# First feed-forward layer of a two-layer network on one core: 68 dense tiles against 24 dense tiles and 39 expert slots in DRAM

## The reference, cut to what matters

```python
probs = softmax(x @ Wr)                       # 8 experts
routing_weights, selected = top_k(probs, 2)   # not renormalised
C = einsum('tk,tke->te', routing_weights, one_hot(selected, 8))
expert_out = vmap(swiglu)(x, Wg, Wu, Wd)      # swiglu: silu(x@wg) * (x@wu) @ wd, 176 hidden columns
moe_out = einsum('te,eth->th', C, expert_out)
shared = swiglu(x, Sg, Su, Sd)                # 704 hidden columns
out = moe_out + sigmoid(x @ Wsg) * shared     # then x = x + tanh(g_ffn[0]) * out
```

## Time and profile before

| | us |
|---|---|
| runs | 876.75, 870.18, 870.32; median 870.32 |
| the profiled execution, device time | 869.0 |
| its span, from first to last instruction | 867.3 |
| TensorE busy in the span | 781.8 (90%) |
| VectorE, ScalarE, GpSimd busy | 566.6, 314.5, 159.2 |

### The profile page before, as it was taken

How to read it: one execution, slowest core, us unless ns; L and a number is a source line. 1 busy time by engine, 2 the same in 40 slices (tenths; PEclk the granted TensorE clock), 3 DMA queues, 4 the chain that set the end, 5 groups by cost and what they waited for, 6 DMA issues and landing times.

```text
span 867.3 us, 13423 instructions
## 1 busy us (share of the span) xinstructions
PE 781.8 (90%) x4612; PEld 634.5 (73%) x4627; DVE 566.6 (65%) x1022; ACT 314.5 (36%) x507; POOL 159.2 (18%) x211
## 2 busy tenths in 40 slices
PE   3887888799999999999997999976699999999994
PEld 2575766688888888888884555545588888888883
DVE  4877778454654574367546898983355876868764
ACT  2220211223423343342234878756143423324221
POOL 2977877300000000021100111111010000000000
PEclk9999999999999999999998999996599999999998
DMA  7221321000000000001001122200000000000000
GB/s 279 73 91 49 104 67 30 1 1 1 1 0 0 0 0 0 0 0 33 19 1 46 54 69 75 60 31 13 1 1 1 2 24 0 0 24 0 24 1 25
DMA packets 22134, 26.09 MB, mean 30 GB/s; under 512 B 5328, under 2 KB 17744, under 8 KB 21968
## 3 DMA queue, kind: packets, MB, share of 16 engines
q1 hardware_dynamic: 22096, 25.60, 9.3%
HBM read 23.22 MB, written 2.10 MB: 29 GB/s over the span
## 4 chain that ended last, share of the span: by engine, by line
PE 70%; DVE 15%; issue 6%; POOL 4%; ACT 2%; SPq 1%; DMA 1%; DVEq 0%; POOLq 0%; ACTq 0%
PE bank L1590 21%; PE bank L1457 19%; PE bank L1470 11%; PE bank L1522 3%; PE bank L1512 3%; POOL A L459 2%; DVE A L874 2%; PE bank L1532 1%; DVE small L1071 1%; PE bank L1599 1%; DVE A L863 1%; POOL R L450 1%; PE bank L1385 1%; PE bank L1504 1%; DVE A L1081 1%
## 5 line engine op out<-in xcount | busy, mean ns | idle before, releaser
L1590 PE MATMUL bank<-R 128*128 128x512 f32 (+3 forms) x1080 | 214.5, 359 | 11.2 <-DVE R L1235 4.9
L1590 PEld LDWEIGHTS bank<-R 128*128 128x128 f32 (+1 forms) x1080 | 181.0, 190 | 44.3 <-DVE R L1235 5.2
L1457 PE MATMUL bank<-R 128*128 128x512 f32 x768 | 186.2, 392 | 1.9 <-issue 1.9
L1457 PEld LDWEIGHTS bank<-R 128*128 128x128 f32 x768 | 140.3, 188 | 29.4 <-issue 2.1
L1019 DVE TENSOR_TENSOR A<-bank,A 128x512 f32<-128x512 f32 (+1 forms) x68 | 47.1, 692 | 114.0 <-PE bank L1457 111.7
L1470 PEld LDWEIGHTS bank<-R 128*128 128x128 f32 (+1 forms) x816 | 105.8, 190 | 10.5 <-issue 4.0
L1470 PE MATMUL bank<-R 128*128 128x256 f32 (+1 forms) x816 | 109.5, 284 | 2.5 <-DVE R L1029 2.2
L595 ACT ACTIVATE A<-bank 128x512 f32<-128x512 f32 (+1 forms) x68 | 40.7, 599 | 189.2 <-PE bank L1457 181.5
L874 DVE TENSOR_TENSOR A<-bank,A 128x512 f32<-128x512 f32 x64 | 43.8, 684 | 20.0 <-PE bank L1375 15.2
L1373 PE MATMUL bank<-A 128*128 128x256 f32 x128 | 40.9, 402 | 14.6 <-DVE A L874 13.6
L766 ACT ACTIVATE A<-bank 128x512 f32<-128x512 f32 (+1 forms) x48 | 28.6, 597 | 64.7 <-PE bank L1590 64.7
(11 more groups left out here) (163 smaller groups left out, 1038.9 us busy)
## 6 DMA issues: line engine op xcount, KB each, us to landing
A<-in_w SPq DMA_DIRECT2D x16, 384.0 KB, 3.1
A<-in_w SPq DMA_DIRECT2D x8, 480.0 KB, 3.6
A<-in_ctx_one SPq DMA_DIRECT2D x8, 272.0 KB, 3.6
A<-in_ctx_half SPq DMA_DIRECT2D x8, 256.0 KB, 3.1
A<-in_ctx_nat SPq DMA_DIRECT2D x4, 512.0 KB, 4.5
A<-in_ctx_t SPq DMA_DIRECT2D x128, 16.0 KB, 2.0
out<-X SPq DMA_DIRECT2D x4, 512.0 KB, 2.9
A<-in_filt SPq DMA_DIRECT2D x1, 1536.0 KB, 11.8
```

The lines of the kernel that those rows point to most:

```text
L1457: mm = nc.tensor.matmul(dst[0:pr], wX[:, j, at + k * P:at + k * P + pr], mX[:, k], start=(n == 0), stop=(n == 5))
L1590: mm = nc.tensor.matmul(dst, a, m, start=start and n == 0, stop=stop and n == len(prods) - 1, skip_group_check=skip)
```

## The change: what it does, and its diff cut to the core

**Routing for all tokens at once.** The shared expert stays dense: 6 tiles per token group, 24 in all, and its sigmoid is now a scale of each token in `b_finish`. Groups are taken in the order 0, 3, 1, 2. Logits of groups 0 to 2 are taken during the last group of stage A and at its end. Once group 3's are there, VectorE ranks them (`rank_step`, 16 steps on 128 columns), TensorE counts positions (`b_positions`, 18 matmuls), and VectorE works out for each token and choice a row in a DRAM buffer (`place_step`, 16 steps; the rows stand after step 11) and for each of 39 slots its expert.

**Slots.** Each expert's tokens take whole slots of 128 rows; 39 slots hold every possible split. GpSimd writes each normed token to its two rows of `xs` by 32 indirect DMAs of 128 rows of 1 KB. For each slot SyncE loads the rows, TensorE transposes them (2), ScalarE and VectorE split them, TensorE multiplies (6 matmuls of 352 columns at a weight address from a register), ScalarE takes silu, VectorE multiplies, TensorE transposes (2), ScalarE and VectorE split, TensorE multiplies (6 of 256), ScalarE copies out, SyncE stores to `ys`. The expert numbers come to TensorE's registers four slots at a time. GpSimd gathers the rows back by 32 more indirect DMAs, and VectorE adds them to X with their weights (`mix_step`).

**Order.** Dense groups 0, 3, 1; all slots; dense group 2 with the clearing of the keys' place (now on VectorE, 16 memsets) and the mixing of token groups 0 and 1; stage C, in whose first two groups VectorE mixes and norms token groups 2 and 3. GpSimd's order at the turn is gather(0), gather(1), root of norm 0, gather(2), root of norm 1, gather(3).

**Stage A** has two `z2` buffers, the sums of a group in two halves during heads 3 and 4 of the next, the skip term batch by batch, and the weights in 14 chunks (12,800 columns against 13,056) split in halves after every second head. SyncE writes zeros over `xs` (5.1 MB) in four transfers. VectorE's loops of stages B and C are written out.

```diff
+NS = 2 * B + E - 1
+ORDER = (0, 3, 1, 2)
+XN_ORDER, XN_AT, TURN_B, TAKE_AT, X_TURNS = (3, 0, 1, 2), (1, 3, 4, 5), (2, 4, 2), (2, 4, 3), 6
+XGS, YSS, GBS = 4, 4, 8
@@ gpsimd
-                if h == 0:
-                    pool.wait_ge(o_ready, 1 + 2 * g)
+                if h == 0 and g >= 2:
+                    pool.wait_ge(o_ready, 1 + 2 * (g - 1))
...
+            pool.wait_ge(where_ready, 1)
+            pool.wait_ge(xs_zeroed, 16 * G)
+            for i in range(G):
+                g = XN_ORDER[i]
+                pool.wait_ge(xn_ready, BG * (i + 1))
+                for t in range(BG * g, BG * (g + 1)):
+                    for r in range(2):
+                        q = r * B + t
+                        nc.gpsimd.indirect_dma_start(xs, bass.IndirectOffsetOnAxis(ap=where[:, q:q + 1], axis=0),
+                                                     XN[:, t], None).then_inc(xs_written, 16)
...
+            pool.wait_ge(edown_done, NS)
+            for u in range(YSS):
+                pool.wait_ge(ys_stored[u], 16 * len(range(u, NS, YSS)))
+            gather(0)
+            gather(1)
...
+            c_root(0)
+            gather(2)
+            c_root(1)
+            gather(3)
@@ sync
+            sp.wait_ge(xs_written, 16 * 2 * B)
+            for n in range(XGS - 1):
+                load_slot(n)
+            for n in range(NS):
+                if n + XGS - 1 < NS:
+                    load_slot(n + XGS - 1)
+                if n >= 2:
+                    store_slot(n - 2)
@@ scalar
+            for n in range(NS + 2):
+                if n + 1 < NS:
+                    e_high_x(n + 1)
+                if n < NS:
+                    e_silu_of(n)
+                if 1 <= n <= NS:
+                    e_high_h(n - 1)
+                if n >= 2:
+                    e_take(n - 2)
@@ vector
+            b_group(2, 0, [])
...
+            for n in range(NS + 1):
+                if n + 1 < NS:
+                    e_low_x(n + 1)
+                if n == 1:
+                    b_finish(2)
+                if n < NS:
+                    e_hidden(n)
+                if n:
+                    e_low_h(n - 1)
+            b_hidden(G - 1, 0)
+            b_group(G - 1, 0, [(1, Steps(clear_step, 16)), (1, mix_and_norm(0)), (1, mix_and_norm(1))])
             b_finish(G - 1)
...
+                    if more and k == 1 and g < 2:
+                        norm = mix_and_norm(g + 2)
@@ tensor
+            def e_gate_up(n, v):
+                pe.wait_ge(xsL_ready, n + 1)
+                if n >= 2:
+                    pe.wait_ge(eh_ready, n - 1)
+                m = 0
+                for xX, wX in ((xsH, wgH), (xsL, wgH), (xsH, wgL)):
+                    for k in range(DT):
+                        mm = nc.tensor.matmul(GU[n % 2][:, 0:F2], xX[:, n % 2, k * P:(k + 1) * P],
+                                              wX[:, bass.ds(v + k * E * F2, F2)], start=(m == 0), stop=(m == 5))
+                        m += 1
+                mm.then_inc(egu_done, 1)
...
+            def e_slots():
+                pe.wait_ge(eid_ready, 2)
+                ids = []
+                for n in range(NS + 2):
+                    if n + 1 < NS:
+                        e_turn_x(n + 1)
+                    if n < NS:
+                        if n % 4 == 0:
+                            ids.append(e_ids(n))
+                        e_gate_up(n, ids[n // 4][0][n % 4])
+                    if n == NS:
+                        b_gate_up(G - 1, 0)
+                    if 1 <= n <= NS:
+                        e_turn_h(n - 1)
+                    if n >= 2:
+                        e_down(n - 2, ids[(n - 2) // 4][1][(n - 2) % 4])
...
+            for i in range(G - 1):
+                b_group(i)
+            e_slots()
+            b_group(G - 1)
+            c_first_q()
```

More of the change, by code:

```diff
@@ new lines, in _ @@
+            dve.wait_ge(a_done, 1 + 2 * G)
+            last = b_norm(G - 1)
+            last.take(2 * BG + 1)
+            b_hidden(0, 0)
+            last.take_all()
+            rank, weigh, place = Steps(rank_step, 16), Steps(weigh_step, 6), Steps(place_step, 16)
+            b_group(0, 0, [(4, rank)])
+            weigh.take_all()
+            b_finish(0)
+            b_hidden(1, 0)
+            b_group(1, 0, [(2, place)])
+            b_finish(1)
+            b_hidden(2, 0)
+            dve.wait_ge(xT_ready, X_TURNS - 1)
@@ L1324, in _ @@
+            c_shift(0, 2)
+            for g in range(G - 1):
                 c_steps(g, True)
-            step.leave(per, G - 1, start)
             c_steps(G - 1, False)
```

1112 lines of the change are left out of this document (688 added, 424 removed).

## The result

The changed kernel takes 878.4 us, the median of 7 runs (872.8 to 882.5), against 870.7 for the kernel before, run beside it: ratio 1.0089, 95% interval [1.0055, 1.0122]. I had forecast 816 (779 to 864), and 0.10 for slower. The profiled execution has a span of 880.8 us in 882.5; my sum had put the span at 812.6. So 68.2 us are to be found, of which some 4 belong to this execution alone: it is 4.1 us over the median. Single runs more than 1.5% above the fastest of their kernel are left out of the medians and ratios here; that concerns two of the four runs of e_half_scatters and one each of e_a_shift and e_root_first.

A forecast was written before the change was run, and what follows sets the result against it. The prediction took TensorE's columns in stage B as the bound. From a span of 867.3 us, 62.7 earlier at stage C's first maximum and 8 longer in stage C gave 812.6; 816 us as device median, range 779 to 864.

The forecast's parts named there:

- Stage A, -13: Stage A: two waits go, 3.4 us gained in each of three groups, 3 net in the last; stage B starts at 151.3.
- the wait for chunk 12: Stage A's bad end, 4 us worse: GpSimd also waits for chunk 12, which ScalarE splits only after a norm.
- The dense groups and the scatter, 99: Stage B before the slots: rows known at 51 us, 32 writes at 1.3, 6.5 for landing, load, turn and split.
- VectorE hindering GpSimd: Stage B and turn: VectorE's two-port modes shut out GpSimd's descriptor making; at the gathers, towards the second, slow-issue rival.
- The dense work's 86 us: Stage B before the slots: three shared-expert groups at 23.7 us plus logits, turns, positions and stalls on TensorE.
- A slot, 2.8: Stage B's 39 slots: TensorE sets the pace, 2.1 us of work plus register costs; 2.8 us each, between 2.1 and 4.3.
- The two register terms, 0.35 each: Per slot on TensorE: 0.35 us for weight addresses from registers, 0.35 for loading the expert numbers.
- The turn, 39: Last slot to stage C's first maximum: copy, store, 16 gathers, root, 8 gathers, root, then VectorE; 39 us.
- Stage C, +8: Stage C: VectorE's 12.2 us of mixes and norms in the first two token groups, partly covered; 8 us longer.
- Stage D: Last stage: untouched by the change, expected at 273 us.
- The rivals: Cheap issues 779 us (0.20); GpSimd's queue, issues 2.1 us, 861 (0.16); slots not overlapping 894 (0.10); half of each 870 (0.04).
- the first rival: Stage B: cheap issues at 0.8 us and slots at TensorE's own pace, 2.3 us; 779 us in total; chance 0.20.

The follow-up runs named there:

- e_half_scatters: Changed kernel with only 16 of the 32 indirect writes, each token's second expert left out; 857.4 us, too few runs for a ratio.
- e_a_shift: Changed kernel with GpSimd's half splits in stage A's last group four heads later; 874.4 us, 1.004 to the kernel before.
- e_root_first: Changed kernel with stage C's second root issued before the third group of eight gathers; 884.1 us, 1.015 to the kernel before.
- e_static_ids: Changed kernel with constant expert numbers, so no loads of them into TensorE's registers; 843.2 us, 0.972 to the kernel before.
- e_dense_first: Changed kernel with the fourth dense group before the slots, first root before the second eight gathers, second mixing in stage C; 890.1 us, 1.021.
- e_plain_pool: Changed kernel with the 32 indirect writes as plain writes to fixed rows from GpSimd's queue, routing left out; 855.7 us, 0.985.
- e_sync_rows: Changed kernel with the 32 writes as plain writes to fixed rows from SyncE's queue, routing left out; 858.5 us, 0.988.
- e_before_32: Kernel before, with 32 indirect writes of a constant tile added where GpSimd is idle; 890.9 us, 1.026.
- e_best_2: Changed kernel with untested expert numbers loaded once before slots, stage A's last half splits later, writes and late gathers spaced, second root first; 827.1 us, 0.951.

## Why the prediction was wrong, point by point

- **What bounds the kernel** was right: TensorE's columns in stage B. 63 us of its work went. The forecast failed in what else it takes to feed it.
- **Stage A, -13, measured +0.7.** From one group's sums to the next it takes 33.5 and 32.6 us, where the kernel before took 34.9 and 33.4: 0.8 to 1.5 us gained and not 3.4. In the later of these groups (90.7 to 123.3 us) GpSimd is busy 27.7 us and VectorE 29.2 of 32.6, so the ring is near its work already. The last group gave it all back. I had named the wait for chunk 12 at the bad end of the range and had taken the middle; e_a_shift shows it worth 3.6 us. The other 10 were not tested.
- **The dense groups and the scatter, 99, measured 122.6: the largest single miss.** Each piece that I had worked out was there: the row numbers 52.6 us into the stage (51), a write every 1.27 us (1.3), landing and first load as priced. The step that failed is the assumption under the sum, that dense work at TensorE's pace goes on beside the writes. The stall accounts for the 23.6 us, shown by plain writes (slots 93.4 us into the stage), by spacing, and in the kernel before; in kernels equal up to there it came to 13.6 us at the least. (A slip of mine beside it: 18 small matmuls by the 16 of the logits are 1.9 us, not 2.5. The dense work's 86 us did not enter the sum.) I weighed one direction only, VectorE hindering GpSimd by the Trainium skill (SBUF — State Buffer, Who interferes with whom); here the hindrance ran the other way and took ScalarE and TensorE too, which share no port with GpSimd by that section; what they all share, no run shows.
- **A slot, 2.8, measured 3.1.** TensorE's own part is 2.23 (2.1 forecast). The two register terms, 0.35 each, are a mis-sized pair: addresses cost next to nothing (46 ns each, and TensorE busy 86.2 of 87.0 us in e_static_ids), loads with their tests 0.87. Without the tests the loads cost some 0.1. The term failed because I priced the call in the source as loads; what it emits besides, sixteen sequencer instructions a batch, was nowhere in my count. The floor of about 600 ns that the Trainium skill gives for a register load (DMA: Bandwidth & Descriptors, Latency and other measured facts) isn't met here: a load of four numbers took 334 ns.
- **The turn, 39, measured 47.7.** The chain is the one forecast, gathers, root, gathers, root, VectorE. It starts later: beside the first sixteen gathers ScalarE starts two silus 2.9 and 7.7 us late (it idles 6.0 and 7.9), VectorE's mixing and first norm stand behind that, and GpSimd waits 7.6 us for them. The same stall, the same failed assumption, for most of the 8.7 us.
- **Stage C, +8, measured +20.6.** The step that failed is that part of the mixing is covered: its clump of VectorE work costs more than its length (8.7 us for 5.8, twice), with TensorE waiting for VectorE and the clock at 0.91. Why was not tested apart; e_dense_first's 15.2 us for 6.4 is no second case, since there the stall has its part.
- **Stage D** was right within 1.5 us.
- **The rivals.** Not one of them happened. GpSimd's issues took 1.27 us and not 2.1; slots overlap; TensorE's own pace of 2.23 us is what the first rival had (2.3), once the tests are gone. The right rival was "the indirect transfers stall the others": no row of before could have given it, since that kernel has no such transfer, and just for that the range should have held a cost for its neighbours and not only for itself. Of the 68.2 us, 23.6 and most of 8.7 lie with the stall. e_plain_pool and e_sync_rows, which have no writes of this kind beside the dense groups, come out at 855.7 and 858.5 us, inside my range.

## What to carry to other kernels

When a change brings in an instruction that the old trace never shows, ask what it does to the others beside it, not only what it costs; the same 32 added to the old kernel, writing to rows that nobody reads, would have told (22 us here; the first ten would have shown nothing). Read what a call emits before pricing it: a range test in TensorE's program cost more than the load it guards. And before moving a wait, look at what it keeps apart or holds back: with the root ahead of the last sixteen gathers the first maximum came 3.9 us sooner, and the kernel lost more than that in stage C.

## What the runs showed of the hardware that I had not expected

- Indirect transfers from GpSimd 1.27 us apart make TensorE, ScalarE and VectorE start instructions late, one of ScalarE's by 18.1 us (it idled 27.6). Eleven writes pass before the first late instruction in the changed kernel, sixteen before the first late by over 1 us in e_before_32, four gathers in e_dense_first. Beside 16 writes ScalarE has 11.6 us of such waits. At 1.47 us apart 10.0 us remain in 32 writes (6.1 in e_best_2); at 2.05 and 2.93 us none. Plain writes of the same bytes, 0.54 us apart on the same queue, do nothing of the kind. In e_before_32 the instruction queues move nothing meanwhile. The cause stays open.
- In TensorE's sequencer the range test's register operation takes 146 ns, an address operation 46 ns, a load of four numbers 334 ns and of one 302 ns.
